# Routed rows kept in token order, with token lists per tile made by one-hot products and rows read by index

## What is computed

```python
# block 0: low-rank layer chosen per batch, then a dense FFN with fake quantisation (I = 704)
t = einsum(x, lora_A[id0]); c = einsum(t, lora_B[id0]) + lang_embed[id0]
x = x + w_down(quant(silu(w_gate(quant(c))) * w_up(quant(c))))
# block 1: adapter chosen per batch, layer norm, then a mixture of 9 experts, the best 2 for each token
h = relu(x @ W1[id1] + b1[id1]) @ W2[id1] + b2[id1]
y = layernorm(x + h) * gamma[id1] + beta[id1]
w, e = top_k(softmax(y @ Wr), 2); w = w / sum(w)
x = x + sum over the token's 2 experts of w * ((silu(y @ Wg[e]) * (y @ Wu[e])) @ Wd[e])
```

## Time and profile before

| | |
|---|---|
| median of 3 runs | 662.99 us (661.88 to 665.92) |
| the profiled execution | 666.66 us |
| its span, first to last instruction | 664.9 us |
| mean granted clock of TensorE | 0.969 |
| busy share | PE 91%, DVE 77%, ACT 67%, POOL 56% |
| HBM | read 44.72 MB, written 24.68 MB |

### The profile page before, as it was taken

One profiled execution on the slowest core, in us unless ns is written; L12 is line 12 of the kernel. 1 busy time (PEld: TensorE's weight loads), 2 busy tenths in 40 slices (PEclk: granted clock), 3 DMA queues, 4 the chain that ended last, 5 costly groups with the idle time before them and its releaser, 6 DMA issues.

```text
span 664.9 us, 16051 instructions
## 1 busy us (share of the span) xinstructions
PE 604.4 (91%) x4404; PEld 412.9 (62%) x4404; DVE 510.1 (77%) x1373; ACT 442.2 (67%) x744; POOL 370.6 (56%) x573
## 2 busy tenths in 40 slices
PE   7988888898985558999999999999999999999994
PEld 2243335676663235777777777777777777777773
DVE  5589995688876879888988888888776666666652
ACT  3657995888864556888877787787665444445542
POOL 4014660047767683666657666667666555555544
PEclk9987999999998879999999999999999999999998
DMA  8524001256557649989899889866775556667552
GB/s 268 199 57 128 1 0 49 83 152 212 197 163 252 186 159 192 235 171 202 182 200 173 189 165 189 182 140 114 158 156 110 112 112 104 119 110 110 101 90 32
DMA packets 157300, 95.67 MB, mean 144 GB/s; under 512 B 107924, under 2 KB 150436, under 8 KB 157220
## 3 DMA queue, kind: packets, MB, share of 16 engines
q1 hardware_dynamic: 142900, 76.12, 47.7%
q0 software_dynamic: 13696, 18.51, 15.8%
q10 hardware_dynamic: 624, 0.03, 0.1%
HBM read 44.72 MB, written 24.68 MB: 104 GB/s over the span
## 4 chain that ended last, share of the span: by engine, by line
PE 55%; DVE 16%; issue 11%; POOL 6%; ACT 4%; DMA 3%; SPq 2%; another core or an unknown queue 1%; POOLq 1%; DVEq 0%; ACTq 0%
PE ps L692 29%; PE ps L743 15%; POOL rows L1643 3%; PE ps L564 2%; DVE big L1524 2%; PE ps L671 2%; DVE big L1364 2%; PE ps L803 1%; DMA small<-small 1%; DVE small L1189 1%; PE ps L582 1%; POOL small L1636 1%; PE ps L559 1%; DMA big<-in_low 1%
## 5 line engine op out<-in xcount | busy, mean ns | idle before, releaser
L692 PE MATMUL ps<-big,small 128*128 x1608 | 251.8, 313 | 2.8 <-ACT big L966 1.4
L692 PEld LDWEIGHTS ps<-big,small 128*128 128x128 f16 x1608 | 157.0, 98 | 81.3 <-issue 4.9
L1681 POOL DMA_INDIRECT out<-small x67 | 110.4, 1648 | 137.7 <-DVE small L1489 131.3
L743 PE MATMUL ps<-big,small 128*128 x1105 | 131.4, 273 | 0.5 <-DMA small<-small 0.5
L743 PEld LDWEIGHTS ps<-big,small 128*128 128x128 f16 x1105 | 105.3, 98 | 12.0 <-issue 0.6
L972 ACT ACTIVATE small<-small 128x704 f16<-128x704 f32 x67 | 52.6, 785 | 77.5 <-DVE small L1464 76.9
L1480 DVE SCALAR_TENSOR_TENSOR small<-small 128x64 f16<-128x64 f32 (+1 forms) x134 | 72.6, 583 | 19.9 <-ACT small L976 19.9
L1464 DVE SCALAR_TENSOR_TENSOR small<-ps,small 128x704 f32<-128x704 f32 x67 | 63.5, 948 | 24.9 <-PE ps L692 23.1
L976 ACT ACTIVATE small<-small 128x704 f16<-128x704 f32 x67 | 59.1, 882 | 28.0 <-DVE small L1474 28.0
L1643 POOL DMA_INDIRECT rows<-small x64 | 66.8, 1044 | 18.0 <-issue 18.0
L1654 POOL TENSOR_SCALAR small<-small 128x1 f32<-128x1 f32 x67 | 71.2, 1063 | 0.0
(11 more groups left out here) (256 smaller groups left out, 1048.7 us busy)
## 6 DMA issues: line engine op xcount, KB each, us to landing
small<-rows SPq DMA_DIRECT2D x67, 130.0 KB
big<-in_Wg SPq DMA_DIRECT2D x8, 704.0 KB, 4.6
big<-in_Wu SPq DMA_DIRECT2D x8, 704.0 KB
big<-in_Wd SPq DMA_DIRECT2D x8, 640.0 KB, 5.1
big<-in_xT SPq DMA_DIRECT2D x8, 512.0 KB, 7.1
small<-in_xT SPq DMA_DIRECT2D x16, 256.0 KB
out<-big SPq DMA_DIRECT2D x16, 256.0 KB
rows<-small SPq DMA_DIRECT2D x13, 130.0 KB, 4.2
```

What stands on the lines that cost most here:

```text
L692: m = e.matmul(ps[:, 2 * j + h, 0:352], xsT_(t)[:, 2 * xp + k, :], bigh[:, bass.ds(o + (4 * j + 2 * wp + k) * I + 352 * h, 352)], start=(n ...
L743: m = e.matmul(ps[:, 7, 0:H], hTE_(t)[:, hc_, :], bigh[:, bass.ds(o + 8 * I + (6 * wp + c) * H, H)], start=(n == 0), stop=(n == len(terms) ...
L1681: e.indirect_dma_start(out=out[:, :], out_offset=bass.IndirectOffsetOnAxis(ap=tok_(t), axis=0), in_=yw_(t), in_offset=None, compute_op=ALU ...
```

## The change

Each token's row is stored once, at its token's place: `Xs` shrinks from 9 regions to 4096 + 256 rows of 259 words (the token number is not stored). `store_rows(b)` is one direct DMA of SP for a batch. The indirect writes go, as do the padding rows behind each expert, all but two spare blocks of rows, `load_rows`, `rowI`, the integer slots, and `side`'s copy of the token number.

The list of tokens of each tile is computed. A token's slot is split into a tile number `q16` and a place 0 to 127 in the tile, `slot8` (POOL, `slot_hot(b)`: four instructions on 8 elements, then eight on 128). For each of the 64 groups of 128 (token, expert) pairs, `lohot` is a one-hot matrix (pair by place) times the pair's token value, and `hot5` / `hot72` (DVE, `hot_first`, `hot_rest`: compares) is a one-hot matrix (pair by tile). The sum of their products on PE (`slots_first`: 48 matmuls with 5 columns, `slots_rest`: 64 with 67 columns) is a table place by tile of token values. `token_rows` (DVE, five instructions) turns it into the row numbers `IT`; places without a token get a row of zeros. POOL's `gather(t)` reads a tile's rows by an indirect DMA with `IT` as index, and `add_rows` uses the same `IT`.

In order: hot_first stands behind positions(6), slots_first behind piece_top(1), token_rows(1) behind piece_scale(1) and ahead of x_lo(0). gather(0) to gather(4) stand behind slot_hot(6) on POOL. hot_rest is in DVE's chunk of t = 0, slots_rest in PE's t = 1 behind proj(1, 1), rest_rows and table_experts in t = 1, table_scales in t = 2. From t = 1 on POOL issues gather(t + 5) ahead of add_rows(t - 3).

```diff
-DUMMY = E * REG
-SPARE = 8
-ROWS = DUMMY + SPARE * P
-PADS = 16 * (2 + SPARE)
-PAY = 260
+NONE = E * REG
+ROWS = T + 2 * P
+PADS = 16 * 4
+PAY = 259
+PAIRS = T * 2 // P
+PER_128 = 1.5 * 2.0 ** 30
...
+        lohot = carve(big, [8 * EW], [PAIRS, P], F16)
+        hot72 = carve(big, [2 * EW], [PAIRS, TILES], F16)
+        hot5 = carve(big, [2 * EW + PAIRS * TILES // 2], [48, SOLO], F16)
...
-            def wait_scattered(b):
-                for t in range(4):
-                    w.wait_ge(f"sc{b % 4}{t}", 32 * use(b, 4))
-
-            def wait_rows():
-                w.wait_ge("pad", PADS)
-                w.wait_ge("pad0", 80)
-                w.wait_ge("pad1", 64)
-                for b in range(last - 3, last + 1):
-                    wait_scattered(b)
+            def store_rows(b):
+                w.wait_ge("route", b + 1)
+                w.wait_ge("aff", 2 * b + 2)
+                e.dma_start(Xs[512 * b:512 * b + 512, :].rearrange("(t p) n -> p t n", p=P), pay[b % 4]).then_inc(S[f"st{b % 4}"], 16)
...
                 elif k < E - 1:
                     w.wait_ge("lo", n - 2 if n >= AHEAD + 3 else 0)
+                    w.wait_ge("slots", 2)
                 else:
                     w.wait_ge("lo", n if j else 0)
-                    wait_rows()
+                    for b in range(last - 3, last + 1):
+                        w.wait_ge(f"st{b % 4}", 16 * use(b, 4))
...
-            def load_rows(t):
-                if t < SOLO:
-                    w.wait_ge("first", 1)
-                    w.wait_ge("hq", hq_after(ST - 1))
-                    w.wait_ge("pd", ST)
-                    lb = 4 if t == 0 else 5
-                    for b in range(lb - 3, lb + 1):
-                        wait_scattered(b)
...
-                v = e.value_load(rowI[0:1, t:t + 1], min_val=0, max_val=ROWS - P)
-                e.dma_start(xs_(t), Xs[bass.ds(v, P), :]).then_inc(S[f"xs{t % 5}"], 16)
...
-            for k in range(SPARE):
-                r = DUMMY + P * k
-                e.dma_start(Xs[r:r + P, :], (padT, padB)[k % 2]).then_inc(S["pad"], 16)
+                e.dma_start(Xs[T + P * k:T + P * k + P, :], padT).then_inc(S["pad"], 16)
...
                 store_x1(i - 2)
+                if i % 2 == 0 and i >= 6:
+                    store_rows((i - 6) // 2)
...
-            load_rows(0)
+            store_rows(6)
             load_piece(3)
-            for t in range(1, SOLO):
-                load_rows(t)
             load_piece(4)
-            w.wait_ge("baseI", 1)
-            for x in range(E):
-                v = e.value_load(baseI[0:1, x:x + 1], min_val=0, max_val=DUMMY - P)
-                e.dma_start(Xs[bass.ds(v, P), :], padT).then_inc(S[f"pad{x % 2}"], 16)
+            store_rows(last)
...
-                for u in range(SOLO, TILES):
-                    if load_at[u] == t:
-                        load_rows(u)
...
                 w.wait_ge("pos", b)
+                if b == last:
+                    w.wait_ge("it", 1)
...
+            def slots_first():
+                w.wait_ge("hot", 1)
+                w.wait_ge("lh", 6)
+                w.wait_ge("pos", NB - 1)
+                for i in range(48):
+                    m = e.matmul(ps[:, 6, 256:256 + SOLO], lohot[:, i, :], hot5[:, i, :], start=(i == 0), stop=(i == 47))
+                m.then_inc(S["slots"], 1)
+
+            def slots_rest():
+                w.wait_ge("lh", NB)
+                w.wait_ge("pos", NB)
+                for k in range(2):
+                    w.wait_ge("hot", k + 2)
+                    for i in range(32 * k, 32 * k + 32):
+                        m = e.matmul(ps[:, 6, 256:256 + TILES - SOLO], lohot[:, i, :], hot72[:, i, SOLO:TILES], start=(i == 0), stop=(i == PAIRS - 1))
+                m.then_inc(S["slots"], 1)
...
             piece_top(1)
+            slots_first()
             keep_busy(14, 0)
...
                     proj(t, 1)
+                if t == 1:
+                    slots_rest()
...
+                if n >= 6:
+                    w.wait_ge("slots", 2)
...
                 w.wait_ge("rt", m_poh)
-                e.tensor_reduce(pk, poh.rearrange("p (a n) -> p a n", n=E), AX, ALU.add).then_inc(S["rt"], 1)
+                w.wait_ge("pq", 4 * b - 4)
+                e.tensor_reduce(pk[b % 2], poh.rearrange("p (a n) -> p a n", n=E), AX, ALU.add).then_inc(S["rt"], 1)
                 m_pk = w.up("rt")
                 w.wait_ge("rt", m_rws)
-                for t in range(4):
-                    w.wait_ge(f"sc{b % 4}{t}", 32 * (b // 4))
+                w.wait_ge(f"st{b % 4}", 16 * (b // 4))
                 e.tensor_tensor(pv[:, :, 257], exd, rws, ALU.mult)
-                e.tensor_scalar(pv[:, :, 259].bitcast(I32), tok4, float(4 * P * b), None, ALU.add)
+                e.tensor_copy(pv[:, :, 256], rws)
                 w.wait_ge("rt", m_pk)
-                e.tensor_copy(posIf[b % 4], pk)
-                e.tensor_copy(pv[:, :, 256], rws)
-                e.tensor_copy(pv[:, :, 258], pk[:, 0:4]).then_inc(S["route"], 1)
+                e.tensor_copy(pv[:, :, 258], pk[b % 2][:, 0:4]).then_inc(S["route"], 1)
+
+            def same_tile(out_, q_, r_, m, n):
+                e.tensor_tensor(out_, q_.rearrange("p (i a) -> p i a", a=1).to_broadcast([P, m, n]),
+                                r_.rearrange("p (a t) -> p a t", a=1).to_broadcast([P, m, n]), ALU.is_equal).then_inc(S["hot"], 1)
+
+            def hot_first():
+                w.wait_ge("first", 1)
+                w.wait_ge("lh", 6)
+                same_tile(hot5, q16[:, 0:48], r16[:, 0:SOLO], 48, SOLO)
+
+            def hot_rest():
+                w.wait_ge("slotF", 1)
+                w.wait_ge("lh", NB)
+                for k in range(2):
+                    same_tile(hot72[:, 32 * k:32 * k + 32, :], q16[:, 32 * k:32 * k + 32], r16, 32, TILES)
+
+            def rest_rows():
+                token_rows(2, SOLO, TILES - SOLO, it72)
+
+            def token_rows(k, at_, n, tmp):
+                v, low_, none_, both = tmp
+                w.wait_ge("slots", k)
+                w.wait_ge("const", POOL_PAD)
+                e.tensor_copy(v, ps[:, 6, 256:256 + n]).then_inc(S["ix"], 1)
+                w.wait_ge("ix", w.up("ix"))
+                e.scalar_tensor_tensor(low_, v, 0.0, v, ALU.is_gt, ALU.subtract)
+                e.scalar_tensor_tensor(none_, v, 0.0, absent[:, at_:at_ + n], ALU.is_equal, ALU.mult).then_inc(S["ix"], 1)
+                w.wait_ge("ix", w.up("ix"))
+                e.tensor_tensor(both, none_, low_, ALU.subtract).then_inc(S["ix"], 1)
+                w.wait_ge("ix", w.up("ix"))
+                e.tensor_scalar(IT[:, at_:at_ + n], both, float(T // 2), None, ALU.add).then_inc(S["it"], 1)
...
-                e.tensor_copy(rowI[:, 0:SOLO], rowF[:, 0:SOLO])
+                e.tensor_scalar(r16[:, 0:SOLO], rowF[:, 0:SOLO], 1.0 / 128, None, ALU.mult)
...
-                e.tensor_scalar(rowF[:, rest], r72[:, rest], row5, float(ROWS - P), ALU.add, ALU.min).then_inc(S["tb"], 1)
+                e.tensor_scalar(rowF[:, rest], r72[:, rest], row5, float(NONE), ALU.add, ALU.min).then_inc(S["tb"], 1)
                 w.wait_ge("tb", w.up("tb"))
-                e.tensor_copy(rowI[:, rest], rowF[:, rest]).then_inc(S["rowI"], 1)
+                e.tensor_scalar(r16[:, rest], rowF[:, rest], 1.0 / 128, None, ALU.mult)
...
             positions(6)
+            hot_first()
             gain(ST - 1)
...
             piece_scale(1)
+            token_rows(1, 0, SOLO, it5)
             x_lo(0)
...
-            chunks = (table_counts, table_rows, table_experts, table_scales)
+            chunks = ((table_counts, table_rows, hot_rest), (rest_rows, table_experts), (table_scales,))
...
-            def scatter(b, half):
+            def slot_hot(b):
                 w.wait_ge("route", b + 1)
-                w.wait_ge("aff", 2 * b + half + 1)
-                for t in range(2 * half, 2 * half + 2):
-                    for k in range(2):
-                        e.indirect_dma_start(out=Xs[:, :], out_offset=bass.IndirectOffsetOnAxis(ap=posI[b % 4][:, k, t:t + 1], axis=0),
-                                             in_=pay[b % 4][:, t, :], in_offset=None).then_inc(S[f"sc{b % 4}{t}"], 16)
+                w.wait_ge("const", POOL_PAD)
+                w.wait_ge("lh", b)
+                e.tensor_scalar(near, pk[b % 2], -63.5, PER_128, ALU.add, ALU.add).then_inc(S["pq"], 1)
+                w.wait_ge("pq", 4 * b + 1)
+                e.tensor_scalar(q128, near, PER_128, None, ALU.subtract).then_inc(S["pq"], 1)
+                w.wait_ge("pq", 4 * b + 2)
+                e.tensor_scalar(q16[:, 8 * b:8 * b + 8], q128, 1.0 / 128, None, ALU.mult).then_inc(S["pq"], 1)
+                e.tensor_tensor(slot8, pk[b % 2], q128, ALU.subtract).then_inc(S["pq"], 1)
+                w.wait_ge("pq", 4 * b + 4)
+                for i in range(8):
```

(45 more changed lines are left out.)

67 lines of the change are left out of this document (26 added, 41 removed).

## The result

| | before | changed |
|---|---|---|
| median of the runs, us | 664.45 (661.88 to 668.71) | 697.72 (696.85 to 702.75) |
| profiled span, us | 664.9 | 701.1 |
| granted clock, mean of the span | 0.969 | 0.954 |

A forecast was written before the change was run, and what follows sets the result against it. ACT and its round trip with PE were taken to pace the second stage, a chain the turn, PE the loop. Terms -2.0 + 10.8 + 5.2 + 1.1 + 1.8 + 0.3 - 2.2 = +15.0 on 663 gave 678 us, range 666 to 690.

The forecast's parts named there:

- What bounds the kernel: Second stage paced by ACT and its round trip with PE, the turn by a chain, the expert loop by PE.
- Step 2: Chain before the first five tiles: slot_hot at 4.4 us and the gather's landing at 3.98 make x_lo(0) later, +10.8 us.
- step 1: Second stage: indirect writes go, the xk load may come in time, slot_hot is hidden by the pace; -2.0 us.
- step 3: Turn: hot_rest's two compares on DVE cost +5.2 us, with slot_hot(7) done by then.
- Steps 3 and 4: Turn: hot_rest on DVE +5.2 us; then rest_rows +1.1 and its wait for slots_rest +1.8.
- Steps 1 and 6: Transfers in time: late xk load in the second stage, 2.0 us; remote wait before times(1) in the turn, 2.2 us.
- Step 5: Start of the loop: table_experts moves before times(1), table_scales from t = 3 to t = 2; +0.3 us.
- Step 7: Expert loop: POOL issues a gather and drops a copy, SP loads no rows; 0 us (0 to +11).
- rival C: Expert loop: POOL becomes late, 5.8 us against 5.66 a tile, some 18 tiles losing 0.6; +11, 689 us; chance 0.15.
- A: Second stage: the indirect writes set the pace after all, so steps fall to 5.25 us; 659 us; chance 0.08.
- B: Turn: it is hidden better, all terms at their low ends; 669 us; chance 0.17.
- D: DMA: pressure is not removed, as gathers and stores return it, so stalls stay; 682 us; chance 0.12.

The follow-up runs named there:

- undisturbed profile: The kernel before, unedited, run and profiled again: profiled span 654.4 us, without any remote wait of DVE; measured 656.15 us.
- experiment 1: Changed kernel with slot_hot's eight compares for batches 0 to 4 issued four behind each of two powers: 683.84 us, 1.040 of the kernel before.
- experiment 3: Run cited: changed kernel with hot_first and hot_rest waiting for q16 alone, not slot_hot's compares: 693.03 us, 1.055 of the kernel before.
- experiment 4: Changed kernel with hot_rest moved behind times(0), slots_rest, rest_rows and the gathers of tiles 5 and 6 to t = 2: 699.16 us, 1.066 of the kernel before.
- mended kernel: Changed kernel with edits such as split compares; with earlier compares, waits for q16 alone and slot_hot(6) behind the gathers: 672.66 us, 1.0075 of the kernel before.

## Why the prediction was wrong

Against the undisturbed profile the stage up to power(14) cost 13.1 us where -2.0 was booked, from there to x_lo(0) 20.1 for 10.8, from there to times(3) 8.1 for 8.4, the loop 5.6 for 0. So the first two failed, and they share one term.

- **What bounds the kernel**: right. The pace of 6.1 to 6.2 us a step holds without the writes (experiment 1; that it is ACT's is argued, no run changed ACT's work), the turn is a chain, the loop is PE's (5.66 per tile late in the loop, before and changed).
- **Step 2, the term of the sum that was mis-sized**: a compare was put at 0.35 us, near the affine select of the earlier trace rows, because it too is one pass over 128. It takes 0.78 to 0.90; a slot_hot 7.4 to 8.2 us and not 4.4, at or beyond the upper end of 7.4, and slot_hot(7), beside DVE's work, 9.9. The row beside it, 0.72 of the two-input power, was the nearer one. This one number was used three times. (a) In step 1, "hidden by the same pace": 4.4 us behind a power would have been, 8.0 are not, in a step of 6.1: +13.1 us at power(14) against the undisturbed profile and +8.2 against the one shown, where -2.0 was booked. The sentence compared POOL's sums per batch (10 us of writes go, one slot_hot comes), though the writes stood four in each step and slot_hot in one of two. (b) Twice in the chain to x_lo(0). (c) In step 3, "slot_hot(7) is done by then": DVE had 8 us of work there, 7 were booked, and hot_rest waited 1.79.
- **Step 2, a wait that was not named as one**: power(14) to x_lo(0) took 5.8 to 10.0 us before and 25.9 after. I let hot_first wait under a stall of 4.45 us ("covered and not gained"). That stall was a remote wait which the undisturbed execution doesn't have, and the wait of hot_first was 7.92, with variance(15), and so power(15), queued behind it: 5.3 us (experiment 3). The landing, taken at 3.98, was 3.0 to 4.9: right; the 2.3 us of the estimate beside it were too short in every profile read.
- **Steps 3 and 4**: right. hot_rest 5.03 us for 5.2; slots_rest 2.24 for 2.2; rest_rows 1.1, its wait 1.75 for 1.8. By the marks the undisturbed profile gives 8.6 - 0.5 = 8.1 from x_lo(0) to times(3), which is the 5.2 + 1.1 + 1.8 that were booked; there is luck in it, since hot_rest's wait of 1.8, which was not booked, and the 2.0 that DVE no longer waits for ACT cancel. That the 5.0 are paid on either side of times(0) is seen in experiment 4.
- **Steps 1 and 6, what falls away**: right in kind, too small. 2.0 and 2.2 us were booked for transfers that come in time, 9.7 fell away against the profile shown. What was not seen is that this is no constant of the kernel: 0 to 16 us in three executions on different chips. Whether the chip makes the difference is not shown.
- **Step 5** (+0.3) is too small to be seen in any run. It named table_experts and table_scales and not table_rows, whose 3.8 us moved ahead of times(0).
- **Step 7 and rival C**: POOL did not become late in the loop. The loop lost 0 to 7 us all the same, through transposes, a mechanism that no rival had. Of what makes a transpose late the gathers are shown as an ingredient, the load of piece 24 is likely, and how they meet in the queues stays open. The 1.8 us that come back behind the last addition are not explained.
- **Rivals**: A and B did not happen, and D (the pressure stays) neither: no profile of the changed or a mended kernel has a remote wait.

## What to carry to other kernels

Work moved to another engine is hidden by the step that it stands in, not by that engine's total: write down what is queued right behind it, when that is wanted, and whether it was spread and is now in one piece. Of an operation with no row of its own take the dearest row of its kind on that engine, or make the answer depend on the price ("hidden up to 5 us"), above all if it enters the sum more than once. And wait for the value that is read, not for the last one that its producer makes.

## What was not expected of the hardware

- GpSimd: 0.78 us for a compare of 128 elements by 128 partitions alone, 0.24 for a copy of the same size, 0.55 for half the elements; DVE 0.26 for the compare.
- Eight of these compares take 6.2 us with DVE idle and 11.75 across a DVE instruction pair of 5.03 us with two inputs; a one-column operation of 0.30 took 4.82.
- The same program of before waits 0, 11.1 or 15.9 us for transfers on DVE up to times(3) in its three profiles (654.4, 664.9 and 670.6 us); the changed one, which writes 18.40 MB and not 24.68, waits 0 in three.
- A transpose issued behind weight loads, with gathers running on POOL's queue, lands after 9 to 12 us in some runs; without the gathers none took over 6.5 us in two profiles.
